# Attention with keys loaded by feature, scores weighed by pair, one masked peaks operation, and widths ahead of the decay sums

## The chip, the cores and the metric

The kernel runs on one core of one Trainium2 chip. The metric is the device time of one execution in microseconds (us); lower is better. Engines are called as the profile calls them: PE (TensorE; PEld its weight loads), DVE (VectorE), ACT (ScalarE), POOL (GpSimd) and SP (SyncE, which issues most DMAs here).

## The reference

32 batches of 512 tokens with 512 features. Each batch goes through a gated attention (an mLSTM in its parallel form) with x, normalised, as queries and a context as keys and values; then all 16,384 rows go through a routed expert network of 8 experts. Only the attention is touched. Cut to what matters:

```python
gi = concatenate([q, k, v], -1)                  # q = layernorm(x); k = v = ctx
ig, fg = gi @ igate_w.T + igate_b, gi @ fgate_w.T + fgate_b
cs = cumsum(log_sigmoid(fg))
log_D = where(tril, cs[:, None] - cs[None, :], -inf) + ig[None, :]
max_log_D = max(log_D, -1)
C = (qh @ kh.T) / 8 * exp(log_D - max_log_D)     # 8 heads of 64
h = C / (max(abs(C.sum(-1)), exp(-max_log_D)) + 1e-6) @ vh
x = x + tanh(g_xattn) * headnorm(h) * out_w
```

## The kernel before

**Tiling.** A batch's 512 tokens are four chunks of 128. Heads go in four pairs of two. Within a chunk the scores are computed in full (`scores`, L738: two heads of 64 rows each side by side in PE, 16 matmuls a pair); between chunks a running state `S` carries keys times values (`chunk_state`, L782; `chunk_states`, L1042). Everything is float32, so keys and queries must be turned by PE (features on partitions) before the scores: `turn` (L668) transposes four 128x128 blocks into one PSUM bank, and ACT copies the bank to `qT` or `kT` (`turned`, L447). The decay matrix of a pair is summed in PSUM by PE (`decays`, L752: masks, climb and peaks), and ACT takes its exponential into `C` (`decay_factors`, L459). DVE multiplies the scores into it (`weighted_scores`, L1023), and PE multiplies the result by the values (`product`, L792). `widths` (L776) spreads the inner factors for the queries that meet the state, and DVE weighs the queries with them (`weighted_queries`, L1033).

**Gates.** `gates` (L702) multiplies qT and kT by the gate weights into one bank; ACT makes log-sigmoids (L524); PE shifts a part of the gates (`shift_gates`, L713); DVE scans (`gate_runs`, L1053), writes "rise" (L1065) from the shift's bank and the ends of the chunks; PE sums these over chunks (`chunk_ends`, L719, two kinds of matmul, L724 and L725); DVE then makes the peaks (`gate_peaks`, L1070): "prior" (L1074, L1075), fall, nr, held, and four operations of 32 partitions that write `peaks`, which hold chunk j's rows in columns of chunk j and zeros elsewhere (L1084). PE's `decays` of the next batch's pair 0 waits for them.

**Order.** The loop runs over i = 0 to 33 and handles several batches at once, staggered: batch i is normalised, b1 = i - 1 is turned and gated, b2 = i - 2 has its scores, b3 is divided and normed on POOL, b4 and b5 get the second layernorm and the router's logits. The order of each engine's work within i is written out by hand, and is the same for every i (PE L814 to L881, ACT L561, DVE L1099, POOL L401, SP L283). In one i, PE runs product 3 of b3, widths 0, the turns q 0, k 0, q 1, k 1, the three chunk states, decays 1, xfT 0 (a turn of the second layernorm's rows), widths 1, scores 1, xfT 1, product 0, xfT 2, q 2, k 2, q 3, xfT 3, k 3, decays 2, widths 2, scores 2, gates, product 1, shift, decays 3, widths 3, chunk_ends, scores 3, logits, product 2, decays 0 and scores 0 of b1, and the turn of the gates.

**Banks.** Four PSUM banks are shared: sides 0 and 1 are T0 and T1, sides 2 and 3 the two halves of `QK`, which the scores also use. The list in `iteration_fills` (L160) says, in PE's order, which fill takes which side and who empties it. A fill waits until the previous occupant of its side has been read (`ahead`, L192), a fill of side 2 or 3 also until the scores there have been weighed (`weighted`, L187: at present per half of a pair, since `weighted_scores` raises "cc" once for each of its two operations), and scores 1 and 2 wait until both halves of QK have been read (`cleared`, L183):

```python
if ahead[kind, b, k]:
    pe.wait_ge(*ahead[kind, b, k])
if (kind, b, k) in weighted:
    pe.wait_ge(*weighted[kind, b, k])
```

**Loads and stores.** SP issues in its own written order (L283): the second half of x for batch i (after ACT's second norm of the batch that held the buffer), the context `kraw` (L290), the store of rows `xfb` (L263), the store of x (L258), probabilities, and the first half of the next x. ACT may overwrite `xfb` only when the row store has landed (L508).

Of the kernel before, what the change touches and what calls it, by code (L numbers as in the profile page):

```python
# [18 lines left out]
FP32 = mybir.dt.float32  # L19
# [9 lines left out]
P = 128  # L29
# [59 lines left out]
def attention(nc, io, NB, dram, sm_all, tg, consts, stored, plan):  # L89

    x_v = io["x"].rearrange("b (j p) e -> b p j e", p=P)
    c_v = io["ctx"].rearrange("b (j p) e -> b p j e", p=P)
    out_v = io["out"].rearrange("b (j p) e -> b p j e", p=P)
    xf_v = dram["xf"].rearrange("(b j p) w -> b p j w", j=TILES, p=P)
    ident, identb, ones = consts["ident"], consts["identb"], consts["ones"]
    with ExitStack() as ctx:
# [57 lines left out]
        s_cd = [sem(f"a_cd{i}") for i in range(VBUF)]  # L154

# [4 lines left out]
        def iteration_fills(i):  # L160
            b1, b2, b5, b6 = i - 1, i - 2, i - 5, i - 6

            plan = [("qw", b2, 0, "dve", 0), ("q", b1, 0, "act", 1), ("k", b1, 0, "act", 2), ("q", b1, 1, "act", 3), ("k", b1, 1, "act", 1),
                    ("st", b2, 0, "act", 0), ("st", b2, 1, "dve", 2), ("st", b2, 2, "dve", 3), ("xfT", b5, 0, "act", 1),
                    ("qw", b2, 1, "dve", 0), ("scores", b2, 1, None, None), ("xfT", b5, 1, "act", 1),
                    ("xfT", b5, 2, "act", 0), ("q", b1, 2, "act", 2), ("k", b1, 2, "act", 3), ("q", b1, 3, "act", 1),
                    ("lt", b6, 0, "dve", 0), ("xfT", b5, 3, "act", 2), ("k", b1, 3, "act", 3),
# [11 lines left out]
        for i in range(NB + 5):  # L179
            pair = 0  # L180
            for kind, b, k, who, side in iteration_fills(i):
# [4 lines left out]
                if side >= 2 and 2 <= i < NB + 2:  # L186
                    weighted[kind, b, k] = (s["cc"], 2 * (PAIRS * (i - 2) + pair) + side - 1)  # L187
# [60 lines left out]
        with nc.Block() as block:  # L248
            @block.sync
            def _(sp):  # L250
# [3 lines left out]

                def store_x2(b):
# [176 lines left out]
            def _(act):  # L432
# [14 lines left out]
                def turned(kind, b, c):  # L447

                    t = filled(act, kind, b, c)
                    act.activation((qT if kind == "q" else kT)[:, b % 2, c, :], t[:, :], ACT.Copy).then_inc(s["ta"], 1)  # L450
# [110 lines left out]
                for i in range(NB + 2):  # L561
# [4 lines left out]
                    if live(b1):  # L566
# [22 lines left out]
                    if live(b1):  # L589
                        turned("q", b1, 2)  # L590
                        turned("k", b1, 2)
# [1261 lines left out]
```

## Time and profile before

| | us |
|---|---|
| median of three runs (3051.99 to 3055.52) | 3052.46 |
| span of the profiled execution | 3051.6 |
| PE busy | 2948.7 (97%) |
| PEld busy | 2395.3 (78%) |
| DVE busy | 1819.7 (60%) |
| ACT busy | 1132.8 (37%) |
| POOL busy | 1065.5 (35%) |

The profiled execution's own time isn't listed apart from the runs; its span lies 0.4 us below the fastest of them, so that little lies around the span, and 0.9 us below their median. Attention fills about the first 930 us and works on all engines; the expert stage behind it is mostly PE. Busy shares of the whole span mix the two. In a timeline a row with a count merges consecutive instructions of one line; "[0.36 <-DVE S L1048]" says that the engine stood idle for 0.36 us before it, until that instruction released it.

### The profile page before, as it was taken

Reading aid. Unit: us, or ns where it says so; the run is one execution under the profiler, and the core shown is the slowest. Engines: PE = TensorE matmul, PEld = TensorE weight load, DVE = VectorE, ACT = ScalarE, POOL = GpSimd, SP = SyncE. Lnnn points to the kernel's source line nnn. Section 1 sums busy time; section 2 is a strip of 40 time slices with the busy share of each in tenths; the row PEclk is TensorE's granted clock in tenths of the full one; section 3 lists DMA queues with packets and bytes.
Section 4 is the critical chain, followed back from the end, with each engine's and each line's share of the span. In section 5 each row is a group of like instructions: output and inputs, shape, how many; then the busy total and the mean of one; then the engine's idle time right before and its main releaser. Section 6 shows DMA issues by size and latency. Waiting matters only on the chain.

```text
span 3051.6 us, 60802 instructions
## 1 busy us (share of the span) xinstructions
PE 2948.7 (97%) x24708; PEld 2395.3 (78%) x24708; DVE 1819.7 (60%) x5124; ACT 1132.8 (37%) x2025; POOL 1065.5 (35%) x1029
## 2 busy tenths in 40 slices
PE   6999999999997599999999999999999999999998
PEld 5888888888886477777777877787787787778886
DVE  6999999999998645354454444444434445444332
ACT  5788788787886211121121121122112122112110
POOL 4777777777776311111122111121112112121111
PEclk9999999999998699999999999999999999999999
DMA  3243444434443412241242132232123214222121
GB/s 122 100 160 120 162 139 149 161 123 165 141 134 113 131 40 37 35 99 31 46 99 48 36 80 35 37 96 62 31 38 93 41 31 111 38 50 57 35 37 24
DMA packets 140575, 250.71 MB, mean 82 GB/s; under 512 B 31968, under 2 KB 31968, under 8 KB 140296
## 3 DMA queue, kind: packets, MB, share of 16 engines
q1 hardware_dynamic: 106296, 170.80, 17.2%
q0 software_dynamic: 28672, 67.65, 12.6%
q10 hardware_dynamic: 5328, 8.36, 0.9%
q8 instruction: 197, 3.23, 0.4%
q14 instruction: 82, 0.67, 0.1%
HBM read 137.23 MB, written 101.19 MB: 78 GB/s over the span
## 4 chain that ended last, share of the span: by engine, by line
PE 64%; DVE 1%; DMA 1%; issue 0%; ACT 0%; POOL 0%; ACTq 0%; DVEq 0%; POOLq 0%
PE DN L1729 32%; PE UP L1700 30%; PE TT L1673 1%; DMA w_raw<-in_L_ffn_W_down 1%; DVE c_hit L1392 0%; PE c_bank L1385 0%; DVE down_lo L1258 0%; PE c_bank L1369 0%; DVE c_hit L1413 0%; ACT z L1643 0%; DVE c_within L1408 0%; ACT down_hi L1252 0%; POOL out_x L1618 0%; DVE c_gained L1445 0%; DVE mid_lo L1761 0%
## 5 line engine op out<-in xcount | busy, mean ns | idle before, releaser
L1618 POOL DMA_INDIRECT out_x<-y,slots x128 | 208.5, 1629 | 1621.1 <-DVE y L1785 1621.1
L1643 ACT ACTIVATE z<-UP,bup 128x512 f32<-128x512 f32 (+1 forms) x352 | 240.8, 686 | 1085.6 <-PE UP L1700 1066.5
L1729 PE MATMUL DN<-down_hi,mid_hi 128*128 128x512 f32 x1408 | 570.8, 405 | 0.0
L1700 PE MATMUL UP<-xT_hi,up_lo 128*128 128x512 f32 (+1 forms) x1408 | 555.5, 395 | 0.0
L1700 PE MATMUL UP<-xT_hi,up_hi 128*128 128x512 f32 (+1 forms) x1408 | 553.5, 393 | 1.8 <-DVE xT_lo L1740 0.9
L1700 PE MATMUL UP<-xT_lo,up_hi 128*128 128x512 f32 (+1 forms) x1408 | 552.0, 392 | 0.0
L1729 PE MATMUL DN<-down_hi,mid_lo 128*128 128x512 f32 x1280 | 505.8, 395 | 0.0
L1729 PE MATMUL DN<-down_lo,mid_hi 128*128 128x512 f32 x1280 | 505.7, 395 | 0.0
L1759 DVE CAST mid_hi<-z 128x512 fp32r<-128x512 f32 (+1 forms) x352 | 151.2, 429 | 486.4 <-ACT z L1643 486.4
L1783 DVE TENSOR_TENSOR y<-DN,bdn 128x512 f32<-128x512 f32 x128 | 88.5, 692 | 432.3 <-PE DN L1729 419.5
L1700 PEld LDWEIGHTS UP<-xT_hi,up_hi 128*128 128x128 f32 (+1 forms) x1408 | 260.3, 185 | 67.5 <-ACT z L1643 2.8
L1700 PEld LDWEIGHTS UP<-xT_lo,up_hi 128*128 128x128 f32 (+1 forms) x1408 | 259.8, 185 | 67.6 <-issue 0.5
L1700 PEld LDWEIGHTS UP<-xT_hi,up_lo 128*128 128x128 f32 (+1 forms) x1408 | 259.9, 185 | 65.5 <-issue 0.5
L1729 PEld LDWEIGHTS DN<-down_hi,mid_hi 128*128 128x128 f32 x1408 | 266.5, 189 | 56.1
L1729 PEld LDWEIGHTS DN<-down_hi,mid_lo 128*128 128x128 f32 x1280 | 240.4, 188 | 58.2
L1729 PEld LDWEIGHTS DN<-down_lo,mid_hi 128*128 128x128 f32 x1280 | 241.1, 188 | 50.1
L1761 DVE TENSOR_TENSOR mid_lo<-z,mid_hi 128x512 fp32r<-128x512 f32 (+1 forms) x352 | 244.1, 693 | 12.1
L1627 ACT ACTIVATE xT_hi<-TT 128x512 fp32r<-128x512 f32 x126 | 68.3, 596 | 467.0 <-PE TT L1673 446.9
L233 POOL TENSOR_TENSOR nsb<-nsb,rr 128x512 f32<-128x512 f32 x125 | 127.0, 1049 | 215.2 <-DVE nn L973 215.2
L1030 DVE SCALAR_TENSOR_TENSOR C<-QK,C 128x512 f32<-128x512 f32 x256 | 164.7, 685 | 8.5 <-PE QK L749 6.5
L749 PE MATMUL QK<-qT,kT 64*128 64x128 f32 x2048 | 146.4, 282 | 13.2 <-DVE S L1048 12.1
L1597 POOL DMA_INDIRECT xg<-rows_scratch,slots x128 | 137.5, 1075 | 56.3 <-issue 38.1
(264 smaller groups left out, 4971.9 us busy)
## 6 DMA issues: line engine op xcount, KB each, us to landing
xs<-in_x SPq DMA_DIRECT2D x64, 512.0 KB, 3.7
kraw<-in_ctx SPq DMA_DIRECT2D x32, 1024.0 KB, 7.3
out_x<-xs SPq DMA_DIRECT2D x32, 1024.0 KB, 12.5
rows_scratch<-xfb SPq DMA_DIRECT2D x32, 1024.0 KB, 10.6
w_raw<-in_L_ffn_W_down SPq DMA_DIRECT2D x40, 512.0 KB, 4.4
w_raw<-in_L_ffn_W_up SPq DMA_DIRECT2D x16, 682.5 KB, 4.1
mid_hi<-mid_hi ACTq DMA_DIRECT2D x32, 86.0 KB
mid_lo<-mid_hi ACTq DMA_DIRECT2D x32, 84.0 KB
```

The costliest lines, as they stand in the source:

```text
L233: ins = eng.tensor_tensor(n, n, spread(scale[:, j, :], 2, DH), ALU.mult)
L749: mm = pe.matmul(QK[:, par, jj], kT[r, b % 2, p, jj], qT[r, b % 2, p, jj], start=True, stop=True)
L1030: dve.scalar_tensor_tensor(out=c, in0=QK[:, par, :], scalar=DH ** -0.5, in1=c, op0=ALU.mult, op1=ALU.mult)\
L1597: pool.indirect_dma_start(xg[:, t, :], None, rows_v, bass.IndirectOffsetOnAxis(ap=slots[:, 4 * n + t:4 * n + t + 1], axis=0)).then_inc(s_r ...
L1618: pool.indirect_dma_start(out_rows, bass.IndirectOffsetOnAxis(ap=slots[:, m:m + 1], axis=0), y[:, t, :], None, compute_op=ALU.add).then_in ...
L1627: act.activation(xT[0][:, c, :], turned(n, c)[:, :], ACT.Copy).then_inc(s["thi"], 1)
L1643: act.activation(z[0:r, k % 2, :], UP[k % 3][0:r, :], ACT.Silu, bias=bup[0:r, e // 2, f:f + 1]).then_inc(s["z"], 1)
L1700: mm = pe.matmul(UP[k % 3][0:r, :], weights.up[wa][:, c, f * P:f * P + r], xT[xa][:, c, :], start=first, stop=(c == CH - 1 and wa == 1))
L1729: mm = pe.matmul(DN[m % 2][:, :], lhs, rhs, start=first, stop=(f == FCH - 1 and lhs is parts[-1][0]))
L1759: dve.tensor_copy(mid[0][0:r, f, :], z[0:r, k % 2, :]).then_inc(s["hi"], 1)
L1761: dve.tensor_tensor(mid[1][0:r, f, :], z[0:r, k % 2, :], mid[0][0:r, f, :].bitcast(FP32), ALU.subtract)\
L1783: dve.tensor_tensor(y[:, t, :], DN[m % 2][:, :], bdn[:, e % 2, :], ALU.add).then_inc(s["yp"], 1)
```

## The change

A second array is made on the host and handed in: the context transposed to (batch, feature, token). SP loads keys by feature from it straight into `kT`, in two halves, and all key turns of PE and their ACT copies go. `gates` waits for the keys' loads instead. `weighted_scores` becomes one operation per pair, and "cc" counts pairs. In `gate_peaks` the four operations of 32 partitions become one of 128x128 into `low` and one of 128x512 that multiplies `low`, repeated over the chunks, by the mask `own`. In PE's order `widths` now stands ahead of `decays` for pairs 1 to 3, decays 1 moves behind xfT 0, and scores 3 moves ahead of chunk_ends. The sides of the banks are assigned anew.

```diff
-            plan = [("qw", b2, 0, "dve", 0), ("q", b1, 0, "act", 1), ("k", b1, 0, "act", 2), ("q", b1, 1, "act", 3), ("k", b1, 1, "act", 1),
-                    ("st", b2, 0, "act", 0), ("st", b2, 1, "dve", 2), ("st", b2, 2, "dve", 3), ("xfT", b5, 0, "act", 1),
+            plan = [("qw", b2, 0, "dve", 0), ("q", b1, 0, "act", 1), ("q", b1, 1, "act", 2),
+                    ("st", b2, 0, "act", 0), ("st", b2, 1, "dve", 3), ("st", b2, 2, "dve", 2), ("xfT", b5, 0, "act", 1),
                     ("qw", b2, 1, "dve", 0), ("scores", b2, 1, None, None), ("xfT", b5, 1, "act", 1),
-                    ("xfT", b5, 2, "act", 0), ("q", b1, 2, "act", 2), ("k", b1, 2, "act", 3), ("q", b1, 3, "act", 1),
-                    ("lt", b6, 0, "dve", 0), ("xfT", b5, 3, "act", 2), ("k", b1, 3, "act", 3),
+                    ("xfT", b5, 2, "act", 0), ("q", b1, 2, "act", 2), ("q", b1, 3, "act", 1),
+                    ("lt", b6, 0, "dve", 0), ("xfT", b5, 3, "act", 3),
                     ("qw", b2, 2, "dve", 1), ("scores", b2, 2, None, None), ("shift", b1, 0, "dve", 1), ("qw", b2, 3, "dve", 1),
                     ("gates", b1, 0, "dve", 0), ("lg", b5, 0, "act", 1), ("turn", b1, 0, "dve", 1)]
...
-                    weighted[kind, b, k] = (s["cc"], 2 * (PAIRS * (i - 2) + pair) + side - 1)
+                    weighted[kind, b, k] = (s["cc"], PAIRS * (i - 2) + pair + 1)
...
+                def load_keys(b, half):
+                    c = slice(half * CH // 2, (half + 1) * CH // 2)
+                    if b >= 2:
+                        sp.wait_ge(s["qk"], PAIRS * (b - 2) + (half + 1) * PAIRS // 2)
+                    sp.dma_start(kT[:, b % 2, c, :], k_v[b][:, c, :]).then_inc(s_kt[half][b % 2], 16)
...
                 sp.dma_start(kraw[:, 0, :, :], c_v[0]).then_inc(s_cd[0], 16)
+                load_keys(0, 0)
+                load_keys(0, 1)
...
                         sp.dma_start(kraw[:, b % VBUF, :, :], c_v[b]).then_inc(s_cd[b % VBUF], 16)
+                        load_keys(b, 0)
+                        load_keys(b, 1)
...
                         sp.dma_start(kraw[:, i % VBUF, :, :], c_v[i]).then_inc(s_cd[i % VBUF], 16)
+                    if 2 <= i < NB:
+                        load_keys(i, 0)
                     store_rows(i - 5)
...
                         load_x(i + 1, 0)
+                    if 2 <= i < NB:
+                        load_keys(i, 1)
...
                         for c in range(2):
-                            turned("q", b1, c)
-                            turned("k", b1, c)
+                            turned(b1, c)
...
-                    wait_taken(pe, "k", b, CH - 1)
+                    wait_taken(pe, "q", b, CH - 1)
+                    for lane in s_kt:
+                        pe.wait_ge(lane[b % 2], 16 * (b // 2 + 1))
...
                         for j in range(TILES - 1):
                             chunk_state(b2, j)
 
-                        decays(b2, 1)
                     if live(b5):
                         turn_rows(b5, 0)
                     if live(b2):
                         widths(b2, 1)
+                        decays(b2, 1)
                         scores(b2, 1)
...
+                        widths(b2, 2)
                         decays(b2, 2)
-                        widths(b2, 2)
                         scores(b2, 2)
...
                     if live(b2):
+                        widths(b2, 3)
                         decays(b2, 3)
-                        widths(b2, 3)
+                        scores(b2, 3)
                     if live(b1):
                         chunk_ends(b1)
-                    if live(b2):
-                        scores(b2, 3)
                     if live(b5):
                         logits(b5)
...
-                    for par in range(2):
-                        c = C[:, 2 * (g % CRING) + par, :]
-                        dve.scalar_tensor_tensor(out=c, in0=QK[:, par, :], scalar=DH ** -0.5, in1=c, op0=ALU.mult, op1=ALU.mult)\
-                           .then_inc(s["cc"], 1)
+                    c = C[:, 2 * (g % CRING):2 * (g % CRING) + 2, :]
+                    dve.scalar_tensor_tensor(out=c, in0=QK[:, :, :], scalar=DH ** -0.5, in1=c, op0=ALU.mult, op1=ALU.mult)\
+                       .then_inc(s["cc"], 1)
...
-                    for j in range(TILES):
-                        rows = slice(QD * j, QD * j + QD)
-                        ins = dve.scalar_tensor_tensor(out=peaks[rows, b % 2, j * P:(j + 1) * P], in0=run[rows, :], scalar=incoming[rows, :],
-                                                       in1=held[rows, 0, :].bitcast(FP32), op0=ALU.max, op1=ALU.subtract)
-                    ins.then_inc(s["xm"], 1)
+                    step(dve.scalar_tensor_tensor(out=low[:, :], in0=run, scalar=incoming, in1=held[:, 0, :].bitcast(FP32),
+                                                  op0=ALU.max, op1=ALU.subtract))
+                    dve.tensor_tensor(peaks[:, b % 2, :].rearrange("p (j n) -> p j n", n=P), spread(low[:, :], 1, TILES),
+                                      spread(own[:, :], 2, P), ALU.mult).then_inc(s["xm"], 1)
```

## Rows read from the trace of the kernel before

**Rows 1.** Busy windows: span, us; each engine's busy us (instructions); PEclk, DMA share, GB/s.
```profile
504.65:533.80 29.15, 28.79 (x489) 24.53 (x487) 27.21 (x78) 23.62 (x47) 21.78 (x23) 1.00 0.45 147
```

**Rows 2.** Timeline of PE in one period: start us, us, engine, line, operation, tiles, count.
```profile
510.69 1.16 PE L749 MATMUL QK<-qT,kT 64*128 64x128 f32 x16 [0.36 <-DVE S L1048]
511.79 0.66 PE L683 MATMUL T<-ident,xfb 128*128 128x128 f32 x4
512.37 1.15 PE L805 MATMUL A<-vc,C 128*64 128x65 f32 x32
...
516.18 0.60 PE L683 MATMUL QK<-ident,xfb 128*128 128x128 f32 x4
516.62 0.63 PE L674 MATMUL QK<-ident,kraw 128*128 128x128 f32 x4
517.18 0.40 PE L760 MATMUL EX<-maskneg,identb 64*64 64x512 bf16 x1
```

**Rows 3.** The same timeline: shift, decays 3, widths 3, chunk_ends, scores 3.
```profile
523.41 0.49 PE L717 MATMUL T<-gsum,shift 128*128 128x128 f32 x2
523.83 0.40 PE L760 MATMUL EX<-maskneg,identb 64*64 64x512 bf16 x1
...
524.82 0.44 PE L779 MATMUL T<-inner,selP 128*128 128x384 f32 x1
525.10 0.30 PE L724 MATMUL T<-ends,later 128*128 128x8 f32 x2
525.25 0.36 PE L725 MATMUL T<-unseen,ident 128*128 128x4 f32 x2
525.54 1.16 PE L749 MATMUL QK<-qT,kT 64*128 64x128 f32 x16
```

**Rows 4.** Timeline of DVE in the same period, from C 0 to the next C 0.
```profile
503.75 1.29 DVE L1030 SCALAR_TENSOR_TENSOR C<-QK,C 128x512 f32<-128x512 f32 x2
...
508.80 1.75 DVE L1048 SCALAR_TENSOR_TENSOR S<-S,gb,QK 128x65 f32<-128x65 f32 x8
...
511.89 1.29 DVE L1030 SCALAR_TENSOR_TENSOR C<-QK,C 128x512 f32<-128x512 f32 x2 [0.16 <-PE QK L749]
...
524.00 0.29 DVE L1065 TENSOR_TENSOR rise<-T,cs 128x128 f32<-128x128 f32 x1 [0.29 <-PE T L717]
...
525.77 0.15 DVE L1074 COPY prior<-T 128x4 f32<-128x4 f32 x1
...
527.12 1.44 DVE L1084 SCALAR_TENSOR_TENSOR peaks<-T,prior,held 32x128 fp32r<-32x128 f32 x4
...
532.91 1.29 DVE L1030 SCALAR_TENSOR_TENSOR C<-QK,C 128x512 f32<-128x512 f32 x2
```

**Rows 5.** Timeline of ACT: the copy of xfT 0, the numerators of pair 0.
```profile
510.78 0.59 ACT L457 ACTIVATE xfT<-T 128x512 f32<-128x512 f32 x1
...
514.38 0.61 ACT L480 ACTIVATE nsb<-A 128x520 f32<-128x520 f32 x1 [1.31 <-PE A L810]
```

**Rows 6.** Timelines of POOL and DVE around 883 us, and line L942's durations.
```profile
883.18 1.18 POOL L246 TENSOR_TENSOR xs<-xs,nsb 128x512 f32<-128x512 f32 x1
...
883.35 1.06 DVE L942 TENSOR_TENSOR sm_all<-ex,sx 128x32 f32<-128x32 f32 x1
...
L942 DVE TENSOR_TENSOR sm_all<-ex,sx x25: 191/191/1062, 181.2 to 883.4; 128x32 f32<-128x32 f32 x25
```

**Rows 7.** Costliest groups of the page: us busy, mean ns, idle before.
```profile
L1761 DVE TENSOR_TENSOR mid_lo<-z,mid_hi 128x512 fp32r<-128x512 f32 (+1 forms) x352 | 244.1, 693 | 12.1
```

**Rows 8.** SP's issue of the row store; DMA issues of the page, us to landing.
```profile
510.40 0.51 SPq L263 DMA_DIRECT2D rows_scratch<-xfb  x1
...
kraw<-in_ctx SPq DMA_DIRECT2D x32, 1024.0 KB, 7.3
...
rows_scratch<-xfb SPq DMA_DIRECT2D x32, 1024.0 KB, 10.6
```

**Rows 9.** Timeline of DVE at the start: statistics of batch 1's second half.
```profile
22.78 1.29 DVE L916 BATCH_NORM_STATS2 st<-xs 128x6 f32<-128x512 f32 x2 [0.68 <-DMA xs<-in_x]
```

More of the change, by code:

```diff
@@ L92, in attention @@
     c_v = io["ctx"].rearrange("b (j p) e -> b p j e", p=P)
+    k_v = io["ctxT"].rearrange("b (c p) s -> b p c s", p=P)
     out_v = io["out"].rearrange("b (j p) e -> b p j e", p=P)
@@ L154, in attention @@
         s_cd = [sem(f"a_cd{i}") for i in range(VBUF)]
+        s_kt = [[sem(f"a_kt{half}{i}") for i in range(2)] for half in range(2)]
         def live(b):
@@ L445, in exponentials, with turned @@
                     act.activation(ex[:, :, :], lt[:, :, :], ACT.Exp).then_inc(s["lex"], 1)
-                def turned(kind, b, c):
-                    t = filled(act, kind, b, c)
-                    act.activation((qT if kind == "q" else kT)[:, b % 2, c, :], t[:, :], ACT.Copy).then_inc(s["ta"], 1)
+                def turned(b, c):
+                    t = filled(act, "q", b, c)
+                    act.activation(qT[:, b % 2, c, :], t[:, :], ACT.Copy).then_inc(s["ta"], 1)
                 def turned_rows(b, c):
@@ L589, in _ @@
                     if live(b1):
-                        turned("q", b1, 2)
-                        turned("k", b1, 2)
-                        turned("q", b1, 3)
+                        turned(b1, 2)
+                        turned(b1, 3)
                     if live(b5):
                         turned_rows(b5, 3)
-                    if live(b1):
-                        turned("k", b1, 3)
                     if live(b2):
@@ L666, in _, with turn @@
                 pe.wait_ge(s["prep3"], 1)
-                def turn(kind, b, c):
-                    src, blocks = (q, None) if kind == "q" else (kraw, b % VBUF)
-                    t = fill(pe, kind, b, c)
+                def turn(b, c):
+                    t = fill(pe, "q", b, c)
                     for j in range(TILES):
-                        rows = q[:, j, :] if kind == "q" else kraw[:, b % VBUF, j, :]
-                        mm = pe.transpose(t[:, j * P:(j + 1) * P], rows[:, c * P:(c + 1) * P], ident[:, :])
+                        mm = pe.transpose(t[:, j * P:(j + 1) * P], q[:, j, c * P:(c + 1) * P], ident[:, :])
                     mm.then_inc(s["tfull"], 1)
@@ L741, in scores @@
                     if g:
-                        pe.wait_ge(s["cc"], 2 * g)
+                        pe.wait_ge(s["cc"], g)
                     for taken in cleared.get((b, p), ()):
@@ L794, in product @@
                     g = PAIRS * b + p
-                    pe.wait_ge(s["cc"], 2 * g + 2)
+                    pe.wait_ge(s["cc"], g + 1)
                     if p == 0:
@@ L822, in _ @@
                         pe.wait_ge(s["q"], b1 + 1)
-                        pe.wait_ge(s_cd[b1 % VBUF], 16 * (b1 // VBUF + 1))
                         for c in range(2):
-                            turn("q", b1, c)
-                            turn("k", b1, c)
+                            turn(b1, c)
                     if live(b2):
@@ L843, in _ @@
                     if live(b1):
-                        turn("q", b1, 2)
-                        turn("k", b1, 2)
-                        turn("q", b1, 3)
+                        turn(b1, 2)
+                        turn(b1, 3)
                     if live(b6):
@@ L850, in _ @@
                         turn_rows(b5, 3)
-                    if live(b1):
-                        turn("k", b1, 3)
                     if live(b2):
+                        widths(b2, 2)
                         decays(b2, 2)
-                        widths(b2, 2)
                         scores(b2, 2)
@@ L1785, in _, with program @@
                         dve.tensor_scalar(y[:, t, :], y[:, t, :], gs[:, n % 2, t:t + 1], None, ALU.mult).then_inc(s["y"], 1)
-def program(nc, x, ctx_, g_x, g_f, igw, igb, fgw, fgb, outw, Wr, br, Wup, bup, Wdown, bdown, out):
+def program(nc, x, ctx_, ctx_T, g_x, g_f, igw, igb, fgw, fgb, outw, Wr, br, Wup, bup, Wdown, bdown, out):
     NB = x.shape[0]
@@ L1791, in program @@
     K = NTOK // NEXP
-    io = dict(x=x, ctx=ctx_, igw=igw, igb=igb, fgw=fgw, fgb=fgb, outw=outw, Wr=Wr, br=br,
+    io = dict(x=x, ctx=ctx_, ctxT=ctx_T, igw=igw, igb=igb, fgw=fgw, fgb=fgb, outw=outw, Wr=Wr, br=br,
               Wup=Wup, bup=bup, Wdown=Wdown, bdown=bdown, out=out)
@@ L1847 @@
         args.append(nc.dram_tensor(f"in_{name}", a.shape, mybir.dt.from_np(a.dtype), kind="ExternalInput").ap())
+        if name == "ctx_1024":
+            by_feature = np.ascontiguousarray(a.transpose(0, 2, 1))
+            arrays["in_ctx_by_feature"] = by_feature
+            args.append(nc.dram_tensor("in_ctx_by_feature", by_feature.shape, mybir.dt.from_np(by_feature.dtype), kind="ExternalInput").ap())
     shape = inputs["x"].shape
```

## The prediction

> **What bounds the kernel now.** I read the busy windows first, then one batch period engine by engine. The expert stage isn't touched. One steady period of attention is 29.15 us and holds 28.79 us of PE, 27.21 of DVE and 23.62 of ACT [rows 1]. PE looks like the bound, with DVE 1.6 behind it. What counts is who waits within the period. PE stops once, 0.36 us ahead of scores 1, for DVE's S: the banks QK hold chunk states 1 and 2 until DVE has taken them [rows 2]. DVE works without a gap from C of pair 0 at 503.75 until S ends at 510.55 [rows 4]. So a cycle runs: DVE from C 0 to S, PE from scores 1 to chunk_ends (L724), DVE from "prior" (gate_peaks, L1074) to the next C 0. In us from C 0: scores 1 starts at 6.94, the shift of the gates at 19.66, "prior" at 22.02, the next C 0 at 29.16 [rows 2 to 4]. Work taken from PE ahead of scores 1 can't shorten this cycle; only what lies on it counts.
>
> **The change, part by part** (times in us from C 0).
>
> Key transposes. Sixteen PE transposes and four ACT copies go per batch. A group of four takes PE 0.44 us (516.18 to 516.62) [rows 2]. Groups 0 and 1 stand ahead of scores 1 and gain nothing there: S is DVE's. Groups 2 and 3 lie behind it: 0.44, and for group 3 0.59 (from xfT 3 to decays 2 it is 1.00 now, 516.18 to 517.18; without group 3 the next one follows after 0.41 or so). PE would need 1.03 less between scores 1 and the shift.
>
> Scores weighed by pair. Two 128x512 operations last 1.29 together [rows 4]. One of 128x1024 reads as many elements and saves one start; I take 0.07, bounds 0 and 0.15. Of the four in a batch one stands between C 0 and S and one between "prior" and the next C 0. Banks of side 2 now come free together with those of side 3, 0.6 later than before; PE reaches them later still (q group 1 at about 2, C 0 done at 1.3), so this costs nothing.
>
> Masked gate peaks. The four 32-row operations take 1.44 [rows 4]. New: one 128x128, about 0.40 with its wait on the operation before it, and one 128x512, which the nearest row of that size has at 693 ns [rows 7], some 0.62 to the next start. 1.44 - 1.02 = 0.42 saved, on the cycle; bounds 0.3 and 0.55.
>
> Widths ahead of decays, pair 1. Decays 1 moves behind xfT group 0 and widths 1, and that group waits for ACT's xfb. The exponential of pair 1 comes later with it, and ACT takes xfT 0 right behind that: done at 7.62 now [rows 5], at about 8.4 then. xfT group 1 uses the same bank T1 and would come at 6.87 + 1.10 = 7.97 [rows 2]: it waits 0.5. Pair 2: widths 2 takes the bank T1 that q group 3 filled. From product 0 to its nsb copy is 2.01 (512.37 to 514.38) [rows 2, 5], then ACT copies xfT 2, q 2 and q 3 at about half a us each: the bank is free 4.3 behind product 0, and PE, from product 0 to there by its own work, needs 3.8: it waits 0.5 again. The decays that covered it now stand behind it. What covers either now is the 1.0 us of decays ahead of widths [rows 3]; gone, ACT's copies are late next. So scores 1 to the shift is 12.72 - 1.03 + 1.0 = 12.7: the shift starts at 6.87 + 12.7 = 19.55, 19.66 now. The key groups' gain is spent.
>
> Pair 3 costs most. Widths 3 takes the bank of the shift, which DVE frees with "rise" (524.00 + 0.29: 0.88 behind the shift's start) [rows 3, 4]. Decays 3 covered that. And chunk_ends, for which DVE's "prior" waits, moves from ahead of scores 3 to behind it. From rise's end it is then 0.14 to widths 3 (as S's end to scores 1), 0.28 to decays 3 (widths to its follower now), 0.99 to scores 3, 1.10 to chunk_ends (as scores 1 to its follower), and 0.55 until that is done (525.10 to 525.61, and the semaphore) [rows 2 to 4]: 3.06, where it is 1.48 now (524.29 to 525.77). Rise ends at 19.55 + 0.88 = 20.43, so "prior" starts at 23.5, 1.5 later. DVE has only widths 3's queries to weigh meanwhile and stands idle for about 1.8 us; behind it on DVE wait peaks, scores 3, inner factors, the turned gates and the next C 0, and PE's decays 0 wait for peaks. From "prior" to C 0 it is 7.14 now, less 0.42 and 0.07: 6.65. **The new cycle: 23.5 + 6.65 = 30.15, 1.0 longer.** Even with both bank waits absent DVE's own sequence sets a floor: C 1 stays at 8.14 [rows 4], and from there to rise DVE gains at most 0.5 (its two merges, and the 0.3 us in which it now waits for the shift), so rise ends no earlier than 20.05 and the period is 29.75, 0.6 longer.
>
> A wait shared with GpSimd. At 883.35 a DVE multiplication of 128x32 with both inputs in SBUF lasted 1.06, not its median of 0.19, and ended 0.05 behind POOL's two-input operation of 883.18 to 884.36 [rows 6]. The new peaks operation reads low and own, both in SBUF, while POOL multiplies nsb by Wo in back-to-back pieces of that length; the old ones read PSUM and one SBUF tile. It waits for what is left of a piece: 0 to 1.18. My positions aren't good to 0.3 us, so I take the middle, **0.6**, on the cycle.
> The Trainium skill has this as a rule (SBUF — State Buffer, "Who interferes with whom"): a DVE instruction with two SBUF inputs contends with a GpSimd instruction that reads SBUF, and whichever issued second blocks entirely. By the rule the sum is 1.0 to 2.2 a batch, without it 1.0; the trace agrees with it (1.06 against 0.19).
>
> Loads. 1 MB of keys a batch more. load_keys(i, 0) stands ahead of the row store on SP and waits for scores 1, done at 8.0; the store is issued at 6.65 now and lands 10.6 later, at 17.25. kraw, issued just before it, lands after 7.3, so 1 MB takes about 3.8 and the keys' half 1.9: 19.2 by that, and 18.2 since kraw's own load starts 1.0 earlier [rows 8]. ACT's second_norm, which overwrites xfb, stands at 19.40: about 0.7 of cover is left, so nothing. load_keys(i, 1) waits for scores 3 with nothing due behind it until the next batch. At the start 2 MB of keys go ahead of x of batch 1, whose statistics already wait for their DMA at 22.78 [rows 9]: at 3.8 a MB some 7 us, of which slack ahead of the gates covers most. I take 2, bounds 0 and 6.
>
> **Sum.** The pattern runs in 31 periods (both batches live): 31 x (1.0 + 0.6) = 49.6, plus 2: 51.6. 3051.6 + 51.6 = 3103.2. The profiled span lies 0.9 below the median of the runs: 3104.
>
> **Rivals.**
> No collision on peaks (a piece just ending): 31 x 1.0 + 2 = 33, so 3085.
> Faster: if "prior" didn't wait for chunk_ends, which needs PE at the shift 1.5 us earlier against DVE, the removed work would count. DVE would set the period: 29.15 less some 1.1 of waits for PE, less 4 x 0.07 and 0.42, about 27.4 to 27.6. 31 x 1.6 = 50 less, 3003. For it: PE loses over 1.8 us a batch. Against: scores 1 hangs on S, and rise on DVE's own sequence.
> No change: bank waits absent and chunk_ends half a us cheaper; 3050 to 3058.
> Row store late: if the keys cost 2 us more in the queue, ACT stands 1.3 ahead of chunk_totals, for which chunk_ends waits; 31 x 0.5 to 1 more, above 3115. The 0.7 of cover speaks against it.
>
> **Chances.** With collision 0.50, without 0.26, late store 0.07: slower 0.83. No change 0.06, faster 0.11. The range takes the slower cases with their bounds: floor 31 x 0.6 = 19, 3071, less the bounds of the merges (31 x 0.2), 3065; top 31 x 2.2 + 6 = 74, 3126. Less than 0.2% (6 us) can't be told from no change.
>
> **What would show it.** In the changed profile: a period of 30 to 31 us; DVE's first gate_peaks operation idle some 1.8 us for PE's L725; widths 3 idle until rise; xfT 1 and widths 2 idle half a us for ACT's copies; the peaks operation lasting 0.7 to 1.9 us and ending on a POOL piece or 0.55 behind it; scores 1 waiting over a us for S; PE's share of the stage near 90%. A period below 29 us, or a "prior" that doesn't wait, makes the forecast wrong.

## The result and the profile after

The changed kernel takes 3098.61 us (median of 4 runs, 3096.95 to 3102.46), the kernel before in the same session 3053.33 (4 runs): a ratio of 1.0144, 95% interval 1.013 to 1.0159. It is slower by 45.3 us.

The head of its page:

```profile
span 3100.7 us, 59461 instructions
...
PE 2907.1 (94%) x24196; PEld 2340.5 (75%) x24196; DVE 1816.9 (59%) x4932; ACT 1078.3 (35%) x1897; POOL 1078.1 (35%) x1029
```

PE has 41.6 us less to do than in the table of before and DVE 2.8 less, yet the span is 49.1 longer. One steady period, to hold beside [rows 1] (busy windows; us, busy us of PE, PEld, DVE, ACT and POOL with their instructions, PEclk, DMA share, GB/s):

```profile
503.60:534.24 30.64, 27.43 (x471) 22.77 (x471) 27.36 (x71) 21.99 (x43) 22.24 (x23) 1.00 0.51 176
```

The period is 30.64 us where it was 29.15, at the same granted clock (1.00), and PE is busy for 27.43 of it where it was for 28.79. Where PE now stands (its timeline, the rows that answer to [rows 2, 3]):

```profile
502.40 1.16 PE L761 MATMUL QK<-qT,kT 64*128 64x128 f32 x16
504.00 0.66 PE L693 MATMUL T<-ident,xfb 128*128 128x128 f32 x4 [0.44 <-ACT xfT L473]
...
508.81 0.45 PE L791 MATMUL T<-inner,selP 128*128 128x384 f32 x1 [0.21 <-ACT qT L466]
...
514.85 0.49 PE L729 MATMUL T<-gsum,shift 128*128 128x128 f32 x2
515.78 0.45 PE L791 MATMUL T<-inner,selP 128*128 128x384 f32 x1 [0.44 <-DVE rise L1070]
...
517.05 1.06 PE L761 MATMUL QK<-qT,kT 64*128 64x128 f32 x16
...
518.28 0.36 PE L737 MATMUL T<-unseen,ident 128*128 128x4 f32 x2
...
523.25 1.16 PE L761 MATMUL QK<-qT,kT 64*128 64x128 f32 x16 [0.63 <-DVE C L1035]
...
531.13 0.66 PE L693 MATMUL T<-ident,xfb 128*128 128x128 f32 x4 [0.95 <-ACT xfb L526]
```

Here are all three waits for banks that the reordering uncovers: xfT group 1 (0.44), widths 2 (0.21), widths 3 for "rise" (0.44). chunk_ends (L736, L737) stands behind scores 3. Three more stops are new: 0.63 ahead of scores 0 for DVE's C 3, 0.30 ahead of the turned gates (L745) for DVE's steps, and 0.95 ahead of xfT 0 for ACT's second norm. DVE in the same period, for [rows 4]:

```profile
503.60 1.22 DVE L1035 SCALAR_TENSOR_TENSOR C<-QK,C 128x1024 f32<-128x1024 f32 x1
...
515.43 0.29 DVE L1070 TENSOR_TENSOR rise<-T,cs 128x128 f32<-128x128 f32 x1 [0.30 <-DVE cs L1065]
...
518.69 0.16 DVE L1079 COPY prior<-T 128x4 f32<-128x4 f32 x1 [1.83 <-PE T L737]
...
520.43 1.63 DVE L1089 TENSOR_TENSOR peaks<-low,own 128x512 fp32r<-128x512 f32 x1
521.99 1.21 DVE L1035 SCALAR_TENSOR_TENSOR C<-QK,C 128x1024 f32<-128x1024 f32 x1
...
525.50 0.19 DVE L948 TENSOR_TENSOR sm_all<-ex,sx 128x32 f32<-128x32 f32 x1
...
526.22 1.23 DVE L1035 SCALAR_TENSOR_TENSOR C<-QK,C 128x1024 f32<-128x1024 f32 x1
```

DVE stands idle for 1.83 us ahead of "prior", and the masked peaks operation lasts 1.63. The 0.30 us ahead of "rise" are put down to DVE's own scan (L1065), but what "rise" waits for is PE's shift: it starts 0.37 behind the start of the shift's last matmul, as it did before, and a row of e11 below names L729. POOL beside it, and then the same four pieces in the kernel before:

```profile
519.18 5.06 POOL L242 TENSOR_TENSOR nsb<-nsb,Wo 128x512 f32<-128x512 f32 x4
```

```profile
527.55 4.61 POOL L240 TENSOR_TENSOR nsb<-nsb,Wo 128x512 f32<-128x512 f32 x4
```

The four pieces of the changed kernel in the view of that line (ns, minimum, median and maximum, and the first and last start):

```profile
L242 POOL TENSOR_TENSOR nsb<-nsb,Wo x4: 1170/1190/1637, 519.2 to 523.1; 128x512 f32<-128x512 f32 x4
```

Alone a piece takes 1.15 us from start to start (4.61 / 4 in the kernel before). The trace has the second piece from 520.32, just ahead of the peaks operation, to 521.51, unlengthened; the peaks operation ends 0.55 behind that, at 522.06. The third piece begins at 521.47, while the peaks operation is under way, and it is the one that lasts 1.64. So in each meeting the one that began second was held up, and the four pieces take 5.06 where they take 4.61 alone: POOL pays too.

PE's waits over the whole run (waiting line, releaser: us in total, times, longest) show that this is the pattern of every batch:

```profile
PE T L693 <- ACT xfT L473: 23.0, 30, 9.2
...
PE T L791 <- DVE rise L1070: 14.6, 31, 1.4
...
PE T L791 <- ACT qT L466: 8.2, 31, 0.7
```

### The profile page after: what moved, and what is told of

It is laid out like the page before. It is cut to its first block, busy times and chain, and to the rows that moved or that the text cites. A ratio compares the mean times of both kernels' runs of the same rounds, so it can differ in the third digit from the quotient of the medians.

```text
span 3100.7 us, 59461 instructions
## 1 busy us (share of the span) xinstructions
PE 2907.1 (94%) x24196; PEld 2340.5 (75%) x24196; DVE 1816.9 (59%) x4932; ACT 1078.3 (35%) x1897; POOL 1078.1 (35%) x1029
## 4 chain that ended last, share of the span: by engine, by line
PE 61%; DMA 2%; DVE 2%; ACT 0%; issue 0%; POOL 0%; ACTq 0%; DVEq 0%; POOLq 0%
PE DN L1733 31%; PE UP L1704 28%; DMA w_raw<-in_L_ffn_W_down 2%; PE TT L1677 1%; DVE c_hit L1396 0%; DVE down_lo L1262 0%; ACT z L1647 0%; PE c_bank L1389 0%; ACT down_hi L1256 0%; PE c_bank L1373 0%; DVE mid_lo L1765 0%; DVE c_hit L1417 0%; DVE c_within L1412 0%; DVE mid_hi L1763 0%; POOL out_x L1622 0%
## 5 line engine op out<-in xcount | busy, mean ns | idle before, releaser
L482 ACT ACTIVATE C<-EX 128x1024 f32<-128x1024 f32 x128 | 130.5, 1020 | 113.7 <-PE EX L783 113.6
L1035 DVE SCALAR_TENSOR_TENSOR C<-QK,C 128x1024 f32<-128x1024 f32 x128 | 156.1, 1220 | 9.5 <-ACT C L482 4.3
```

The lines of the kernel that those rows point to most:

```text
L482: act.activation(C[:, first:first + 2, :].rearrange("t r (a n) -> t r a n", a=2), EX[:, :, :].rearrange("t a (r n) -> t r a n", r=2), ACT. ...
L1035: dve.scalar_tensor_tensor(out=c, in0=QK[:, :, :], scalar=DH ** -0.5, in1=c, op0=ALU.mult, op1=ALU.mult)\
```

## The experiments

Beside the medians I use the period: the time from one batch's `tm` copy (L1020 before, L1026 after) to the next. It is the same to 0.03 us in most batches of a kernel, so a part's price can be read to a few hundredths. Longer single batches are told apart. The periods are of one profiled execution each, the ratios of the medians of 4 to 11 runs of the kernel.

| kernel | period | ratio to before, 95% |
|---|---|---|
| before | 29.15 | 1 |
| changed | 30.64 | 1.013 to 1.0159 |
| before, only the new order (e4) | 31.51 | 1.0215 to 1.0251 |
| before, only masked peaks (e10) | 29.51 | 1.0023 to 1.005 |
| changed, old order (e3) | 29.28 | 1.0013 to 1.0033 |
| changed, old peaks (e11) | 30.17 | 1.0088 to 1.0121 |
| changed, old order and old peaks (e12) | 28.80 | 0.9964 to 0.9986 |
| changed, chunk_ends ahead of scores 3 (e1) | 30.50 | 1.0115 to 1.0153 |
| changed, `low` in PSUM (e2) | 30.06 | 1.0074 to 1.011 |
| changed, peaks and probabilities in PSUM (e7) | 30.02 | 1.0075 to 1.0108 |
| e7 with the old order (e6) | 28.42 | 0.9923 to 0.9961 |
| e6, gate factors earlier on ACT (e8) | 28.35 | 0.9905 to 0.9949 |
| changed, keys loaded for two batches only (e9) | 30.65 | 1.0117 to 1.0151 |
| e12, keys loaded behind the burst (e13) | 28.80 | 0.9962 to 0.9982 |

### The order of PE's work

e3_old_order: the changed kernel, decays ahead of widths again and chunk_ends ahead of scores 3.

```diff
                             chunk_state(b2, j)
+                        decays(b2, 1)
...
                         widths(b2, 1)
-                        decays(b2, 1)
                         scores(b2, 1)
...
-                        widths(b2, 2)
                         decays(b2, 2)
+                        widths(b2, 2)
...
-                        widths(b2, 3)
                         decays(b2, 3)
-                        scores(b2, 3)
+                        widths(b2, 3)
                     if live(b1):
                         chunk_ends(b1)
+                    if live(b2):
+                        scores(b2, 3)
```

> The changed kernel with PE's order of decays, widths, scores 3 and chunk_ends as in the kernel before; keys still loaded, scores still weighed by pair, peaks still masked. Theory (the new order is the loss): the two waits for ACT's copies and for rise vanish behind decays, prior comes at about 21 us from C 0 instead of 23.4, the period is 27.9 to 29.0 with what the shared wait costs, 3014 to 3048: faster than the kernel before. Rival (loads, or PE idling, cost the time): it stays above 3080. Rival (the removed PE work was never worth anything): it comes back to the kernel before, 3053.

Measured: 3059.31 us, period 29.28. The order costs 1.36 us a batch. That is the theory's cause, but less than the 1.6 to 2.7 that its period of 27.9 to 29.0 asks for, and 3059 lies above its range: what was thought to be a gain of the rest is none. DVE's timeline says why:

```profile
523.26 0.16 DVE L1080 COPY prior<-T 128x4 f32<-128x4 f32 x1
...
525.01 0.69 DVE L1090 TENSOR_TENSOR peaks<-low,own 128x512 fp32r<-128x512 f32 x1
525.62 1.22 DVE L1036 SCALAR_TENSOR_TENSOR C<-QK,C 128x1024 f32<-128x1024 f32 x1
527.24 0.35 DVE L1097 TENSOR_SCALAR held<-T,lows 128x128 fp32r<-128x128 f32 x1 [0.41 <-ACT T L568]
...
529.65 1.12 DVE L949 TENSOR_TENSOR sm_all<-ex,sx 128x32 f32<-128x32 f32 x1
```

"prior" waits for only 0.12 us, and the masked operation, which now starts 1.1 us ahead of POOL's L242 (526.10), lasts 0.69. The masked form wins 0.46 from "prior" to C 3. But DVE then waits 0.41 for ACT, whose turned gates (L568) now come later than DVE does, and the product of the probabilities (L949, 0.19 when alone), again with both inputs in SBUF, lasts 1.12.

e4_before_new_order: the kernel before with the reverse of that diff, so the new order with the key turns, the old peaks and two operations for the scores.

> The kernel before with only PE's order changed as the change does it (widths ahead of decays for pairs 1 to 3, decays 1 behind xfT 0, scores 3 ahead of chunk_ends). Theory: prior moves back by 1.6 us through the tail and by up to 1.2 through the later decays 1, so 1.6 to 2.8 us a batch, 3103 to 3140. Rival (the loss comes from the loads or from the masked peaks): 3053 to 3065.

Measured: 3124.01 us, 31.51, within the range. The order alone adds 2.36. PE's timeline:

```profile
515.98 0.66 PE L683 MATMUL T<-ident,xfb 128*128 128x128 f32 x4 [0.80 <-ACT xfT L457]
...
528.25 0.44 PE L779 MATMUL T<-inner,selP 128*128 128x384 f32 x1 [0.44 <-DVE rise L1064]
```

Against the changed kernel without its masked peaks (e11, 30.17) the key turns and the two operations cost 1.34 here. So the change's 1.49 is a walk of three steps: the order +2.36 (before to e4), the loaded keys and merged scores -1.34 (e4 to e11), the masked peaks +0.47 (e11 to the changed kernel). The removed work is worth 1.34 only where the order has put PE's waits on the cycle; under the old order it is worth 0.35 (e12, below). The new sides of the banks were never tried alone. They aren't the loss: e4 has the old sides and is slow, e12 the new ones and isn't.

e1_ends_first: only the last pair of the order undone.

```diff
                         widths(b2, 3)
                         decays(b2, 3)
-                        scores(b2, 3)
                     if live(b1):
                         chunk_ends(b1)
+                    if live(b2):
+                        scores(b2, 3)
```

> The changed kernel with chunk_ends put back ahead of scores 3, nothing else. Theory (a late chain through the gates): DVE's prior starts 1.1 us earlier in a batch (one step of scores, 1.10), so the period falls from 30.64 to about 29.5 and the time by 31 x 1.1 = 34, to 3065; unless a two-input DVE operation further on (the probabilities' product) now falls on a POOL piece, which takes back up to 1.0 of it and leaves 3090. Rival (the 1 MB more of loads a batch costs the time, or PE idling): the order of two PE steps moves nothing, 3095 to 3102.

Measured: 3092.99 us, 30.50.

```profile
509.98 0.16 DVE L1080 COPY prior<-T 128x4 f32<-128x4 f32 x1 [0.93 <-PE T L737]
...
511.72 1.40 DVE L1090 TENSOR_TENSOR peaks<-low,own 128x512 fp32r<-128x512 f32 x1
...
516.57 1.19 DVE L949 TENSOR_TENSOR sm_all<-ex,sx 128x32 f32<-128x32 f32 x1
```

This is the exception that the expectation named. The wait for chunk_ends fell by 0.90 and the masked operation by 0.23, 1.13 together; the product of the probabilities went from 0.19 to 1.19 and left 0.14. The gain was there and was lost to the next operation that shares with POOL.

### The masked peaks

e11_rows_peaks: the changed kernel with the four 32-row operations of before in place of the two new ones (the diff of `gate_peaks`, backwards).

> The changed kernel with only the masked peaks undone (four operations of 32 partitions again, which read PSUM). Theory of the shared wait: low and peaks take 2.02 us from L1087 to the next C in the changed kernel, the four took 1.44, so the period falls by 0.58 from 30.64, less some 0.1 for the product of the probabilities, which comes nearer to POOL's piece: 30.1 to 30.2, about 3082 to 3086. Rival, that the lost 1.49 us are all in the new order: the four are slower by 0.42 than the masked ones, 31.06, 3112.

Measured: 3086.74 us, 30.17. The period is as the shared wait has it, the time 0.7 us above its range and far from the rival's.

```profile
539.24 0.29 DVE L1070 TENSOR_TENSOR rise<-T,cs 128x128 f32<-128x128 f32 x1 [0.30 <-PE T L729]
...
543.85 1.43 DVE L1089 SCALAR_TENSOR_TENSOR peaks<-T,prior,held 32x128 fp32r<-32x128 f32 x4
...
548.85 0.19 DVE L948 TENSOR_TENSOR sm_all<-ex,sx 128x32 f32<-128x32 f32 x1
```

The masked form costs 0.47 us a batch where it was to save 0.42. e12_old_order_rows_peaks is e3 with the same edit; of the change only the loads and the merged scores are left.

> The changed kernel with PE's old order and the old peaks; what is left of the change is the loads and the scores weighed by pair. Against e3_old_order the four peaks operations are 0.42 us longer. If a wait absorbs it (in e3 the product of the probabilities lasted 1.12 and ended with a piece of POOL), that product is shorter by 0.4 and the period stays at 29.28: 3059. If not, 29.7 and 3072. A period of 29.15 or less would say that loads and merge do bring something by themselves.

Measured: 3047.01 us (ratio 0.9964 to 0.9986), period 28.80, so neither theory's 29.28 or 29.7, and by the third reading the loads and the merge do bring something by themselves, 0.35 us a batch. "Rise" and "prior" hardly wait there (0.03 and 0.14 us): the cycle runs through DVE's own work, and what PE no longer does counts for little. Of the two theories the first had seen the product of the probabilities get shorter (1.12 to 0.63), but not that the wait for ACT goes too. C 3 to the inner factors takes 1.55 where it took 2.01 in e3. So the masked form wins 0.46 and loses 0.46 and 0.49: 0.49, and the periods differ by 0.48.

```profile
526.00 1.44 DVE L1090 SCALAR_TENSOR_TENSOR peaks<-T,prior,held 32x128 fp32r<-32x128 f32 x4
527.46 1.22 DVE L1036 SCALAR_TENSOR_TENSOR C<-QK,C 128x1024 f32<-128x1024 f32 x1
529.01 0.90 DVE L1101 TENSOR_TENSOR inner<-T,held 32x128 fp32r<-32x128 f32 x3
...
531.02 0.63 DVE L949 TENSOR_TENSOR sm_all<-ex,sx 128x32 f32<-128x32 f32 x1
```

e10_before_masked: the kernel before with nothing but the masked peaks (that diff forwards).

> The kernel before with one part of the change, the masked gate peaks. Without a wait shared with POOL the period falls by the 0.42 us forecast, 29.15 to 28.73, and 31 of them give 13 us less: about 3041. Theory of the shared wait: in the kernel before POOL's first piece of nsb times Wo starts within 0.1 us of where the masked operation would; if that piece goes first the operation lasts up to 1.9 and the period is 29.2 to 29.9: 3055 to 3077. If the gain is absorbed further on, by the product of the probabilities (L942 here), that one shows 0.5 to 1.1 us and the period stays near 29.15: 3053.

Measured: 3063.89 us, 29.51, inside the second range and by the third's mechanism. In the plain batches the operation takes its 0.69, and what is won goes twice:

```profile
562.64 0.69 DVE L1084 TENSOR_TENSOR peaks<-low,own 128x512 fp32r<-128x512 f32 x1
563.25 1.28 DVE L1030 SCALAR_TENSOR_TENSOR C<-QK,C 128x512 f32<-128x512 f32 x2
564.76 0.35 DVE L1091 TENSOR_SCALAR held<-T,lows 128x128 fp32r<-128x128 f32 x1 [0.23 <-ACT T L552]
...
567.16 0.69 DVE L942 TENSOR_TENSOR sm_all<-ex,sx 128x32 f32<-128x32 f32 x1
```

From "prior" to C 3 0.47 is won. Then `held` (L1091), waiting for ACT, starts 1.51 behind C 3, where it was 1.21, and the probabilities take 0.50 more. In a few batches the peaks lasted 1.3 to 1.7 as well (four periods are 30.7), and the measured time contains these too. In all three settings the masked form lost 0.36 to 0.48 us a batch.

e2_peaks_psum: `low` written into unused columns of the gates' bank, so that the masked operation has one input in PSUM.

```diff
-                    step(dve.scalar_tensor_tensor(out=low[:, :], in0=run, ...))
+                    step(dve.scalar_tensor_tensor(out=t[:, P:2 * P], in0=run, ...))
-                    ... spread(low[:, :], 1, TILES), ...
+                    ... spread(t[:, P:2 * P], 1, TILES), ...
```

> The changed kernel with the first of the two peaks operations writing to free columns of the gates' PSUM bank instead of low in SBUF, so that the 128x512 one has one SBUF input. Theory (a wait shared with GpSimd): the operation takes 0.69 us instead of 1.63, the period falls by up to 0.94, to 29.7, and the time by 28, to 3070; a later two-input operation may collide instead and leave half, 3085. Rival (the masked operation is long because it reads with two broadcasts): it stays at 1.6 us and 3098.

Measured: 3080.93 us, 30.06, between the theory's 3070 and the 3085 of its exception.

```profile
509.38 0.69 DVE L1089 TENSOR_TENSOR peaks<-T,own 128x512 fp32r<-128x512 f32 x1
...
513.51 0.57 DVE L948 TENSOR_TENSOR sm_all<-ex,sx 128x32 f32<-128x32 f32 x1
```

The same elements and the same mask take 0.69 in place of 1.63, in every batch but the first (0.91), so 0.94 of them were waiting; this is the direct proof that the place of the input decides, and the rival of the two broadcasts is out. Of the 0.94 the probabilities took 0.38.

e7_no_collision: e2, and the reciprocals of the probabilities into PSUM too, with that product moved ahead of the inner factors.

```diff
                 def inner_factors(b):
...
+                    if live(b - 5):
+                        dve.wait_ge(s["lex"], b - 4)
+                        step(dve.tensor_reduce(sx[:, :], ex[:, :, :], AX.X, ALU.add))
                     dve.wait_ge(s["into"], b + 1)
+                    if live(b - 5):
+                        r = t[:, P:P + TILES]
+                        step(dve.reciprocal(r, sx[:, :]))
+                        dve.tensor_tensor(sm_all[:, (b - 5) * TILES:(b - 4) * TILES, :], ex[:, :, :], spread(r, 2, NEXP), ALU.mult).then_inc(s["smx"], 1)
```

> The changed kernel, PE's order as in it, with no two-input SBUF operation left on DVE's path while POOL works: the first peaks operation writes to PSUM, and the probabilities' reciprocal too, with its product moved ahead of the inner factors. Theory (0.9 a batch from the new order, 0.6 to 0.9 from the wait shared with GpSimd): the product takes 0.2 us instead of the 0.57 of the kernel with PSUM peaks alone, the period is 29.7 us and the time 3068: still slower than before, by what the order costs. Rival (the shared wait is all of the loss): 3053.

Measured: 3081.46 us, 30.02, above the 3068 and 29.7 of the theory and far from the rival's 3053.

```profile
510.44 0.69 DVE L1089 TENSOR_TENSOR peaks<-T,own 128x512 fp32r<-128x512 f32 x1
...
512.60 0.19 DVE L1102 TENSOR_TENSOR sm_all<-ex,T 128x32 f32<-128x32 f32 x1
```

Both operations have their plain durations (0.69 and 0.19), but the moved one delays the steps for which PE turns the gates (0.84 of PE's waiting there, 0.30 before), and C 3 to the next C 0 became 4.46 us from 4.23. A better place for it wasn't tried, so that this is the reason for the missing 0.3 us is argued and not shown.

### Without the new order

e6_no_coll_old_order is e7 with e3's order; e8_gates_early is e6 and on ACT:

```diff
+                    if live(b1):
+                        gate_factors(b1)
                     if live(b5):
                         logit_rows(b5)
                     if live(i):
                         first_norm(i, (0,))
-                    if live(b1):
-                        gate_factors(b1)
```

> The same, and PE's order of decays, widths, scores 3 and chunk_ends as before the change. Theory: the old order alone left a period of 29.27 us in which the probabilities' product stood 1.12 us on a POOL piece; without that and with part of DVE's 0.41 us wait ahead of the inner factors filled, 28.4 us and 3032, below the kernel before. Rival (the removed key transposes buy nothing with DVE as bound, and the product's wait only hides another): 3053 to 3060.

> The kernel of the old order without collisions, and ACT's gate factors put ahead of the logits' copy and the first quarter of the norm, so that DVE's inner factors find them ready. Theory: 0.25 to 0.4 us a batch less again, 28.1 us and 3020 to 3025. Rival (another wait, ACT's in-order wait for peaks, takes its place): no better than without this edit.

Measured: e6 3038.46 us (3030.65 to 3040.06), period 28.42 as forecast, its median 6 us above; e8 3032.09 (3024.78 to 3036.69), 28.35. e8's edit brought 0.07 us a batch of the 0.25 to 0.4 forecast, since DVE then waits 0.30 for PE's turned gates and 0.23 for chunk_ends, and by their times e8 and e6 can't be told apart. Both beat both kernels. e7 and e6 differ by the order alone: 1.60 us a batch. The prediction's rival "faster" needed a "prior" that doesn't wait. Once the order and the shared waits are gone this is nearly so (0.12 us in e6), and the kernel is faster, but by half of what the rival had: 28.4, not 27.4 to 27.6.

### The loads

e9_keys_once:

```diff
-                    if 2 <= i < NB:
-                        load_keys(i, 0)
...
-                    if 2 <= i < NB:
-                        load_keys(i, 1)
...
-                        pe.wait_ge(lane[b % 2], 16 * (b // 2 + 1))
+                        pe.wait_ge(lane[b % 2], 16)
```

> The changed kernel with keys by feature loaded for the first two batches only; all later batches compute with those keys, so it leaves out 30 of the 32 key loads of 1 MB and its output differs. Theory (the loads are hidden): the same time as the changed kernel, 3095 to 3101. Rival (the row store behind the keys' half, or the traffic, costs time each batch): down by 0.3 us or more a batch, 3089 or less.

Measured: 3094.0 us, 30.65: 1 us below the range of the first theory, and not as low as the rival's 3089. In the steady period the loads cost nothing. In these two profiles they cost something in single batches. In the changed kernel three batches took 31.37, 32.86 and 32.90 us, and none of e9's takes over 30.89. In e12, four took 32.8 to 34.6. PE's and the DMA's views of one of them (e12, 456 to 460 us; DMA engines' busy tenths and packets, and queue: packets, MB, share):

```profile
458.01 1.15 PE L817 MATMUL A<-vc,C 128*64 128x65 f32 x30
461.25 0.27 PE L817 MATMUL A<-vc,C 128*64 128x65 f32 x2 [2.09 <-issue]
...
DMA  9999999999999999999999999999985421221000
...
q8 instruction: 1, 0.02, 1.5%
```

PE stops inside one block of matmuls for 2.09 us with nothing to wait for, the DMA engines are full until 459, and a packet of an instruction queue lands in that window. In e3, e12 and e13 the gap lies at the same instruction of the same batch (30 of 32 matmuls done), as it would if the code's blocks were what comes late.

The traces tie these stops to that queue more closely. From 100 us to the last `tm` the fourteen kernels have 26 stops of PE of over 0.55 us without a recorded wait. Each of the 26 ends 1.24 to 1.62 us behind the end of a 16,384-byte instruction packet of q8: here the packet ends at 459.75 and PE goes on at 461.25. There are 108 to 112 such packets in a kernel's stretch, so by chance one stop in twenty would fall so. That PE waits for its instructions in these stops is thus well supported; that the full DMA engines are what makes them late is not shown.

e13_keys_after_burst: both halves of the keys behind the first half of x.

```diff
-                    if 2 <= i < NB:
-                        load_keys(i, 0)
                     store_rows(i - 5)
...
                     if 2 <= i < NB:
+                        load_keys(i, 0)
                         load_keys(i, 1)
```

> e12_old_order_rows_peaks with the keys' first half loaded behind the first half of x, beside the second, so that it no longer lies in the burst of context, rows and out_x (in e12 the DMA engines are 99% busy from 449 to 459 us, PE stands still in the middle of the products of pair 1 from 459.2 to 461.25, waiting for nothing that the profile shows, and a packet of the instruction queue lands near the end of that burst). Theory: instructions are fetched late behind the longer burst. Then the four batches of 32.8 to 34.6 us in e12's profile are gone, its span falls by up to 18 us and the median of the runs by 5 to 12: 3035 to 3042. Rival: the gaps have nothing to do with where the keys are loaded; a few batches of over 32 us stay, and the median is e12's, 3047 (the plain period, 28.8 us, is the same by both).

Measured: 3046.55 us against e12's 3047.01: no difference, as the rival has it. The gap at that instruction is there still, and shorter:

```profile
461.09 0.27 PE L816 MATMUL A<-vc,C 128*64 128x65 f32 x2 [1.11 <-issue]
```

After batch 3 its batches of over 30 us have 30.1 to 30.9 us, where e12's had 32.8 to 34.6, but the median doesn't follow. Whether the transfers ahead of the packets make them late, and how much the stops cost in a typical run, stays open.

## Why the prediction was right

**The sum.** Forecast 3104 with a range of 3065 to 3126, chance of slower 0.83; measured 3098.61. Within the periods the profile grew from 943.0 - 39.7 = 903.3 us to 987.3 - 39.5 = 947.8 (first to last `tm`), 44.5 where 49.6 was forecast. The remaining 4.6 of the span's 49.1 lies behind the last batch's `tm` (2113.4 us against 2108.6); that stretch lies between 2107.2 and 2113.4 in the kernels here, without a pattern that I can name. The sum has no term for it, so that it brings the span's growth nearer to the 51.6 of the forecast is luck.

**The cycle, point by point**, from C 0 (526.22 - 30.64 = 495.58) as the prediction counts it:

| | before | forecast | after |
|---|---|---|---|
| scores 1 | 6.94 | 6.87 | 6.82 |
| shift | 19.66 | 19.55 | 19.27 |
| rise ends | 20.54 | 20.43 | 20.14 |
| "prior" | 22.02 | 23.5 | 23.11 |
| next C 0 | 29.16 | 30.75 | 30.64 |

From row to row the change adds -0.12, -0.27, -0.01, +1.49 and +0.39: what is lost is lost between "rise" and the next C 0.

- *Key turns spent on bank waits.* Right. Scores 1 to the shift is 12.45, forecast 12.7. xfT 1 waits 0.44 for ACT (0.5 forecast), widths 2 only 0.21 (0.5 forecast): that term was more than twice too large.
- *Pair 3.* Right, and the main cost. From rise's end to "prior" it is 2.97, forecast 3.06, before 1.48. DVE's idle time is 1.83, forecast 1.8. e3 against the changed kernel, and e11 against e12, give the whole new order as 1.36 and 1.37, e6 against e7 as 1.60. What each pair costs by itself wasn't separated: e1 undoes the last pair alone, but the shared wait took its gain.
- *The wait shared with GpSimd.* Right in kind, short in size: 0.94 a batch, forecast 0.6 within 0 to 1.18. Here the page of the Trainium skill that the prediction named (SBUF — State Buffer, "Who interferes with whom") states that a DVE instruction with two SBUF inputs contends with a GpSimd instruction that reads SBUF. The case agrees: two SBUF inputs 1.63 us, one of them moved to PSUM 0.69. What the forecast lacked is that such a wait isn't tied to one operation. Whatever brings DVE forward there lets the probabilities' product run into the next piece: e1, e2, e3, e10.
- *"Prior" to C 0.* 7.53 measured, 6.65 + 0.6 = 7.25 forecast; with 0.94 for the shared wait it would have been 7.59.
- *Masked peaks save 0.42.* The step is right by the durations (0.69 alone, and e10 wins 0.47 up to C 3), but the masked form cost 0.36 to 0.48 in each of the three settings. The prediction's two numbers for it, -0.42 and +0.6, gave +0.18.
- *Scores by pair.* 1.22 in place of 1.29: the 0.07 taken.
- *Loads at no cost in the period.* Right (e9). The store of the rows lands sooner than forecast, and the second norm behind it doesn't wait:

```profile
kT<-in_ctx_by_feature SPq DMA_DIRECT2D x64, 512.0 KB, 5.6
...
rows_scratch<-xfb SPq DMA_DIRECT2D x32, 1024.0 KB, 9.0
```

  Half a MB of keys takes 5.6 us from issue. The rows are issued later than before (534.65, 8.4 behind C 0, where it was 6.65) and land 9.0 behind that, at 17.4 where 18.2 to 19.2 was forecast. The single long batches weren't foreseen.
- *A sign that didn't come.* Scores 1 was to wait over a us for S. It waits 0.09: PE stands 0.95 at xfT 0 for ACT just ahead of it instead. S still sets when scores 1 starts (it ends at 532.94, scores 1 starts at 533.04), so the cycle doesn't change by this.
- *The start.* 2 us forecast, some 0.3 measured at the first scan of batch 1, and none at the first `tm` (39.5 against 39.7). The statistics of batch 1 wait for their load, where before it was 0.68 [rows 9], but the scan behind them starts at 30.84. In the changed kernel:

```profile
25.46 2.64 DVE L922 BATCH_NORM_STATS2 st<-xs 128x6 f32<-128x512 f32 x4 [8.15 <-DMA xs<-in_x]
...
30.84 0.42 DVE L1065 TENSOR_TENSOR_SCAN cs<-T,low 128x128 f32<-128x128 f32 x1 [0.68 <-ACT low L550]
```

  and in the kernel before, where that scan waited 2.47 for ACT:

```profile
30.58 0.42 DVE L1060 TENSOR_TENSOR_SCAN cs<-T,low 128x128 f32<-128x128 f32 x1 [2.47 <-ACT low L534]
```

So the total was right because the cycle was. That it came so near is partly luck: two errors of the sum go against each other (the shared wait 0.34 too low, the stretch from scores 1 to the shift 0.25 too high).

## What to carry to other kernels

When three engines hand work round a ring, write the ring down with its times and ask of each edit whether it lies on it: here a removal of 1.36 us of PE's work a batch, with the merged scores, brought 0.35 (e12), and another order of the same work cost 1.4. A block that PE works on while a bank it needs next is still being read is cover; before it is moved, list every bank it gives time to. And a gain on an engine that shares a wait with another one must be followed to the end of the ring, since the next shared operation can take it back; an operand in PSUM ended the wait of each operation that got one.

## What the runs showed that I had not expected

- A DVE operation with both inputs in SBUF (128x512) beside POOL's pieces of 1.15 us took 1.63 us against 0.69, and a 128x32 one 0.57 to 1.19 against 0.19. POOL's four pieces became 5.06 us from 4.61. With one input in PSUM the 128x512 operation took 0.69 (e2) and the 128x32 one 0.19 (e7).
- The loss moves in steps: DVE earlier by 1.13 us gained 0.14 (e1), by 0.94 gained 0.58 (e2), by 0.47 lost 0.36 (e10).
- In a ring with no other disturbance the period repeats to 0.03 us over some 25 batches, which makes it a finer measure than the medians (0.1 to 0.3%).
- PE stands still for 0.6 to 2.1 us at the same few instructions in kernels that load the keys, with the DMA engines 85% busy or more in the 10 us before it. In the three that load no keys, or those of two batches alone (e4, e10; e9), no such gap of over 0.6 us shows in the attention stage; the kernel before has one of 0.85. Every one of the 26 ends 1.24 to 1.62 us behind an instruction packet. What makes the packets late was not settled.
